# Differential attention on one core: maxima transposed into another bank, values read where the projection left them, squares of the differences on GpSimd

## The reference, cut to what matters

```
Q, K, V = X @ Wq, X @ Wk, X @ Wv            # per head 16 wide; Q, K split into two maps of 8
A1, A2  = Q1 K1^T / sqrt(8), Q2 K2^T / sqrt(8)   (causal)
attn    = softmax(A1) - lam[h] * softmax(A2)
O       = attn @ V                           # 16 wide per head
O       = O / sqrt(mean(O * O) + eps) * rms_scale * 0.2
out     = O @ Wo
```

## Time and profile before

| | us |
|---|---|
| median of 3 runs | 445.51 |
| lowest, highest | 442.61, 448.01 |
| the profiled execution's time | 446.8 |
| its span, first to last instruction | 445.1 |

### The profile page before, as it was taken

The page is one execution under the profiler, slowest core; times in us unless marked ns, Lnnn a source line. Parts: engine busy times, 40 slices in busy tenths (PEclk is TensorE's granted clock), DMA queues, the critical chain, the costliest instruction groups (busy, mean ns, idle before and its releaser), DMA issues.

```text
span 445.1 us, 10136 instructions
## 1 busy us (share of the span) xinstructions
PE 377.5 (85%) x3380; PEld 243.8 (55%) x3380; DVE 288.7 (65%) x952; ACT 259.4 (58%) x634; POOL 203.6 (46%) x324
## 2 busy tenths in 40 slices
PE   0699688795999988888888799897888999999996
PEld 0566487672555545545454455443685566655674
DVE  6586363484889797988889697111132989999200
ACT  3333134133788787787968687877367434343832
POOL 5232224002558575675747475834002687783000
PEclk9999799895999999999999999959899999999999
DMA  8789969984554445152535400000000000000011
GB/s 211 251 275 327 260 145 211 169 157 81 76 74 74 74 75 75 41 91 39 84 45 76 73 4 3 4 1 0 0 2 2 0 0 2 0 0 1 2 48 47
DMA packets 47347, 34.51 MB, mean 78 GB/s; under 512 B 20032, under 2 KB 41664, under 8 KB 47296
## 3 DMA queue, kind: packets, MB, share of 16 engines
q1 hardware_dynamic: 47296, 33.86, 37.2%
HBM read 25.20 MB, written 8.39 MB: 75 GB/s over the span
## 4 chain that ended last, share of the span: by engine, by line
PE 41%; DVE 18%; ACT 11%; issue 11%; DMA 7%; POOL 6%; SPq 5%; DVEq 0%; POOLq 0%
PE ps L1268 5%; PE ps L1088 5%; ACT arena L820 4%; PE ps L1010 4%; DVE arena L1402 3%; DMA stacks<-arena 3%; PE ps L644 3%; DMA qk_parts<-qk_parts_sb 3%; PE ps L1259 2%; PE ps L1018 2%; DVE arena L1415 2%; PE ps L1164 2%; SPq L407 2%; PE ps L1005 2%; PE ps L1134 2%
## 5 line engine op out<-in xcount | busy, mean ns | idle before, releaser
L772 POOL TENSOR_SCALAR_AFFINE_SELECT arena<-arena 128x256 f32<-128x256 f32 (+1 forms) x192 | 90.5, 485 | 88.3 <-ACT arena L820 84.7
L820 ACT ACTIVATE arena<-ps 128x512 f32<-128x512 f32 x192 | 109.3, 604 | 28.7 <-PE ps L1044 27.3
L953 DVE TENSOR_REDUCE arena<-ps 128x4 f32<-128x1024 f32 x64 | 78.2, 1221 | 14.2 <-PE ps L1018 12.9
L946 DVE CUSTOM_DVE_ANT_0 ps<-ps,future 128x128 f32<-128x128 f32 x256 | 66.4, 320 | 22.2 <-PE ps L1005 21.9
L1044 PE MATMUL ps<-stacks 50*128 50x256 bf16 x256 | 50.9, 281 | 1.4 <-ACT arena L820 1.3
L1343 POOL TENSOR_TENSOR arena<-arena 128x1024 f32<-128x1024 f32 x16 | 34.2, 2137 | 34.3 <-DVE arena L1428 33.8
L1010 PE MATMUL ps<-stacks 48*128 48x256 bf16 x256 | 41.7, 277 | 3.4 <-ACT arena L820 2.0
L472 POOL TENSOR_TENSOR qk_parts_sb<-qk_rest,qk_parts_sb 128x512 bf16<-128x512 f32 x16 | 19.1, 1209 | 49.8 <-DVE qk_parts_sb L557 49.8
L1088 PE MATMUL ps<-arena 128*17 128x256 f32 x512 | 41.8, 400 | 0.0
L1005 PE MATMUL ps<-stacks 48*128 48x128 bf16 x256 | 25.3, 220 | 16.2 <-DMA stacks<-arena 7.2
L1471 PE MATMUL ps<-arena,upto 128*128 128x384 f32 x96 | 36.0, 487 | 0.0
(11 more groups left out here) (129 smaller groups left out, 765.0 us busy)
## 6 DMA issues: line engine op xcount, KB each, us to landing
stacks<-qk_parts SPq DMA_DIRECT2D x96, 128.0 KB, 4.5
qk_parts<-qk_parts_sb SPq DMA_DIRECT2D x16, 384.0 KB, 4.5
arena<-in_L_ffn_fc_B_dram SPq DMA_DIRECT2D x4, 1024.0 KB, 8.0
arena<-in_L_ffn_fc_A_dram SPq DMA_DIRECT2D x16, 256.0 KB, 4.8
xs<-in_L_attn_a_X_dram SPq DMA_DIRECT2D x4, 256.0 KB, 3.9
qk_parts<-qk_parts_sb SPq DMA_DIRECT2D x8, 128.0 KB, 5.1
stacks<-arena SPq DMA_DIRECT2D x64, 4.0 KB
out_dram<-xs SPq DMA_DIRECT2D x4, 256.0 KB, 2.3
```

What stands on the lines that cost most here:

```text
L772: nc.gpsimd.affine_select(out=diag, in_=diag, compare_op=ALU.is_ge, fill=0.0, base=0, pattern=[[0, 2 if s < 2 else UMAPS], [1, P]], channe ...
L820: nc.scalar.activation(probs[:, r, s, :], ps[:, bank, :], ACT.Exp, scale=SCALE).then_inc(exp_done, 1)
L946: last = nc.vector.tensor_tensor_reduce(out=block, in0=block, in1=future[:], scale=1.0, scalar=LOWEST, op0=ALU.add, op1=ALU.max, accum_out ...
L953: nc.vector.tensor_reduce(out=rowmax[:, gs, 1, UMAPS * uu:UMAPS * (uu + 1)], in_=ps[:, S_BANK + 1:S_BANK + 3, :].rearrange("p b (m k) -> p ...
```

## The change

The transposed maxima go to columns 256 to 511 of bank 6 (for the first group still to bank 7). With this the wait of L1134 for `shift_lo` goes, and stands ahead of the products of the next slot (slots 1 and 5), which write bank 6. L1112 waits for the copy out of bank 6 (L838) in place of the one out of bank 7 (L847). The copy of the values is dropped and TensorE reads `values`. The squares are a product on GpSimd in slot 2, behind that slot's masks, and the division by 16 is the scale of the Ln.

In order: the lag of the squares; the new home; `attend_gpsimd`, behind the subtraction; `attend_scalar`, where `squares` and its two calls go too; `weigh_values` at t = 0; and `emit` of `attend_tensor`, at the transposes of the maxima and then of the products.

```
-L_DEN, L_DIFF, L_SQ, L_MS, L_ROOT, L_NORM, L_OPT, L_OPROJ, L_STAT = 16, 17, 19, 19, 20, 21, 22, 23, 23
+L_DEN, L_DIFF, L_SQ, L_MS, L_ROOT, L_NORM, L_OPT, L_OPROJ, L_STAT = 16, 17, 18, 19, 20, 21, 22, 23, 23
...
+        def maxima_home(it, j):
+
+            if not past(group(it, j, L_SHIFT)):
+                return ps[0:GMAPS, M_BANK, 0:SEQ]
+            return ps[0:GMAPS, O_BANK + 1, SEQ:2 * SEQ]
...
+                b = seq(it, j, L_SQ)
+                if (j - L_SQ) % UPS == 0 and live(b, SEQS):
+                    pool.wait_ge(post, FIRST + 4 * b + 4)
+                    if past(b):
+                        pool.wait_ge(nT_done, FIRST + b)
+                    nc.gpsimd.tensor_tensor(o_n, o1, o1, op=ALU.mult).then_inc(sq_done, 1)
...
-                b = seq(it, j, L_VAUG)
-                if (j - L_VAUG) % UPS == 0 and live(b, SEQS):
-                    if past(b - 1):
-                        act.wait_ge(pv_done, UPS * (b - 1))
-                    nc.scalar.copy(vaug[:, (j - L_VAUG) // UPS % 2].rearrange("p t h d -> p t (h d)"),
-                                   values[:, bass.ds(TPS * b, TPS), :, :].rearrange("p t h d -> p t (h d)"))\
-                        .then_inc(vaug_done, 1)
...
-                    nc.scalar.activation(msum, msum, ACT.Ln, bias=eps[:, 0:1]).then_inc(ms_log, 1)
+                    nc.scalar.activation(msum, msum, ACT.Ln, scale=1.0 / DV, bias=eps[:, 0:1]).then_inc(ms_log, 1)
...
-                    if jj % UPS == 0:
-                        pe.wait_ge(vaug_done, seq(it, j, L_PV) + 1)
+                    g = group(it, j, L_SHIFT)
+                    if (j - L_SHIFT) % UPG == 1 and live(g, GROUPS):
+                        pe.wait_ge(shift_lo, g + 1)
...
-                    if past(shifts_before(it, j)):
-                        pe.wait_ge(shift_lo, shifts_before(it, j))
-                    transposes_copied(it, j)
+                    if past(g):
+                        pe.wait_ge(shift_lo, g)
+                    if past(unit(it, j, L_PV)):
+                        pe.wait_ge(ot_copied, unit(it, j, L_PV))
...
-                    if (j - L_SHIFT) % UPG == 0 and live(g, GROUPS):
-                        pe.wait_ge(shift_lo, g + 1)
```

More of the change, by code:

```diff
@@ L31 @@
 DV = 2 * DH
-ROOT_OF_INV_DV = 0.25
 MAPS = 2 * HEADS
@@ L68 @@
 PROBS = 4
-L_SHIFT, L_EXP, L_PV, L_OT, L_VAUG = 4, 6, 8, 9, 5
-L_DEN, L_DIFF, L_SQ, L_MS, L_ROOT, L_NORM, L_OPT, L_OPROJ, L_STAT = 16, 17, 19, 19, 20, 21, 22, 23, 23
+L_SHIFT, L_EXP, L_PV, L_OT = 4, 6, 8, 9
+L_DEN, L_DIFF, L_SQ, L_MS, L_ROOT, L_NORM, L_OPT, L_OPROJ, L_STAT = 16, 17, 18, 19, 20, 21, 22, 23, 23
 def live(index, count):
@@ L167, in hybrid_kernel @@
         b2, at = carve(at, (KR, D))
-        vaug, at = carve(0, (2, TPS, HEADS, DV + 1))
-        rowmax, at = carve(at, (2, TPS, GMAPS))
+        rowmax, at = carve(0, (2, TPS, GMAPS))
         shift, at = carve(at, (2, SHIFT_ROWS, SEQ), BF16, GMAPS)
@@ L661, in project_tensor @@
             pe.wait_ge(v_done, SEQS)
-        vaug_done = sem("vaug_done")
         cleared = sem("cleared")
@@ L717, in seq @@
             return (SLOTS // UPS) * it + (j - lag) // UPS
-        def shifts_before(it, j):
-            return (SLOTS // UPG) * it + (j - L_SHIFT - 1) // UPG + 1
+        def maxima_home(it, j):
+            if not past(group(it, j, L_SHIFT)):
+                return ps[0:GMAPS, M_BANK, 0:SEQ]
+            return ps[0:GMAPS, O_BANK + 1, SEQ:2 * SEQ]
         def attend_sync(sp):
@@ L824, in emit @@
                         if s == 0:
-                            squares(it, j)
                             inverse_root(it, j)
@@ L893, in shift_high @@
                         act.wait_ge(shift_in[(k - 2) % 4][h], 32 * (it + (k - 2) // 4 + 1))
-                nc.scalar.activation(shift[:, k % 2, 0, :], ps[0:GMAPS, M_BANK, 0:SEQ], ACT.Copy,
+                nc.scalar.activation(shift[:, k % 2, 0, :], maxima_home(it, j), ACT.Copy,
                                      scale=-1.0).then_inc(shift_hi, 1)
@@ L916, in shift_low @@
                     nc.vector.scalar_tensor_tensor(
-                        out=shift[:, k % 2, 1, :], in0=ps[0:GMAPS, M_BANK, 0:SEQ], scalar=-1.0,
+                        out=shift[:, k % 2, 1, :], in0=maxima_home(it, j), scalar=-1.0,
                         in1=shift[:, k % 2, 0, :], op0=ALU.mult, op1=ALU.subtract).then_inc(shift_lo, 1)
@@ L1075, in weigh_values @@
                 jj = j - L_PV
-                p, r, v = jj % PROBS, jj % 2, jj // UPS % 2
+                p, r, tile = jj % PROBS, jj % 2, TPS * seq(it, j, L_PV) + t
                 if t == 0:
@@ L1087, in weigh_values @@
                     if t == 0:
-                        nc.tensor.matmul(ps[32 * m:32 * m + DV + 1, O_BANK + r, 0:SEQ], vaug[:, v, 0, head, :],
+                        nc.tensor.matmul(ps[32 * m:32 * m + DV + 1, O_BANK + r, 0:SEQ], values[:, tile, head, :],
                                          probs[:, p, m // 2, m % 2 * SEQ:m % 2 * SEQ + SEQ],
@@ L1092, in weigh_values @@
                         last = nc.tensor.matmul(ps[32 * m:32 * m + DV + 1, O_BANK + r, P:SEQ],
-                                                vaug[:, v, 1, head, :], probs[:, p, 2, m * P:(m + 1) * P],
+                                                values[:, tile, head, :], probs[:, p, 2, m * P:(m + 1) * P],
                                                 start=False, stop=True, skip_group_check=True)
@@ L1107, in emit @@
                     pe.wait_ge(maxed, BANKS_U * UPG * (g + 1))
-                    if past(shifts_before(it, j)):
-                        pe.wait_ge(shift_lo, shifts_before(it, j))
-                    transposes_copied(it, j)
+                    if past(g):
+                        pe.wait_ge(shift_lo, g)
+                    if past(unit(it, j, L_PV)):
+                        pe.wait_ge(ot_copied, unit(it, j, L_PV))
                     for t in range(TPS):
-                        last = nc.tensor.transpose(ps[0:GMAPS, M_BANK, t * P:(t + 1) * P],
+                        last = nc.tensor.transpose(maxima_home(it, j)[:, t * P:(t + 1) * P],
                                                    rowmax[:, k % 2, t, :], ident[:])
@@ L1120, in emit @@
                 if live(n, UNITS):
-                    g, b = group(it, j, L_SHIFT), seq(it, j, L_OPT + 1)
-                    if (j - L_SHIFT) % UPG == 0 and live(g, GROUPS):
-                        pe.wait_ge(shift_lo, g + 1)
+                    b = seq(it, j, L_OPT + 1)
                     if (j - L_OPT - 1) % UPS == 0 and live(b, SEQS):
```

## The result

| | us |
|---|---|
| before, median of 20 runs | 444.49 (440.82 to 448.01) |
| after, median of 20 runs | 447.07 (442.85 to 450.41) |
| ratio after to before | 1.0062, 95% interval 1.0037 to 1.0086 |
| forecast, over 445.5 | 447.8, +2.25 |

The change costs 2.6 us by the medians, 0.6%. The interval leaves out 1, so it is slower here, but by little. (Ratios leave out the runs over 1.5% above the fastest of their kernel; the medians have all.) The profiled execution after has a span of 443.9 us against 445.1 before, so the two traces can't be subtracted from each other as wholes; they are compared stretch by stretch.

The account below looks back on a forecast made before the run. The loop was taken as bound by VectorE's gapless shift and maxima plus the shift transfer, not L1134. Terms -0.3 - 2.0 + 3.0 + 0.9 + 0.65 = +2.25 us gave 447.8 us; range 440.5 to 452.5.

Parts of the forecast that it names:

- the clock: Whole run: a half-clock stretch gone or added moves the time some 4 us either way; counted only in the range.
- the squares: Product on GpSimd in slot 2 comes late: +3.0 us in six sequences, +0.9 and +0.65 us in the last two.
- the two gains: New bank -0.3 us and dropped copy of the values -2.0 us, together -2.3 us.
- The bank: L1134's removed wait starts no step of the loop earlier; -0.3 us, for the first groups.
- The values: Copies on ScalarE go, 0.31 us in slot 6 of three sequences and more early on: -2.0 us, bounds 0 and -4.8.
- The squares in the loop: GpSimd's square, taken as 1.27 us, delays L934, then L916 and the transfer: +3.0 us for six sequences, bounds 0 and +5.
- The cover ahead of slot 6: Some 0.3 us of each loss from the late square is taken up ahead of slot 6; bounds 0 and 0.5.
- The tail: Seventh sequence: L872 waits for L934, which waits for GpSimd, +0.9 us; eighth: 1.27 in place of 0.63, +0.65.
- Rival 1: L1134's removed stall was on the path: about 432.5 us; chance 0.07.
- Rival 2: GpSimd's square ends before L934's old start, only the gains are left: about 442 us; chance 0.13.
- Rival 3: GpSimd becomes the bound in slots 2 to 5; each 0.1 us more costs 0.8, 452.8 us at 1.9; chance 0.18.
- the masks of slot 3: GpSimd's masks, needed by slot 5's products, come 1.27 us later with 0.5 us of cover; more would stop slot 5.

Follow-up runs that it names:

- second measurement: The changed kernel timed again against the kernel before, beside three versions with moved statistics: 447.01 us, ratio 1.0024 (0.9980 to 1.0069).
- e1_bank: The kernel before with the new bank for the transposed maxima alone: 443.22 us, ratio 0.9961 (0.9927 to 0.9996).
- e9: New bank and values read directly, squares on ScalarE, new statistics moved from slot 7 to slot 6 of the next sequence; against the kernel before 438.40 us, ratio 0.9852.
- e4_bank_values: The changed kernel with the squares back on ScalarE in slot 3, bank and values as changed; against the kernel before 443.43 us, ratio 0.9932.
- e2_values: The kernel before with the copy of the values dropped alone: 440.75 us, ratio 0.9910 (0.9875 to 0.9944).
- e10: Values read directly and statistics moved to slot 6, squares on ScalarE, without the new bank; against the kernel before 437.39 us, ratio 0.9851.
- e3_squares: The kernel before with the squares on GpSimd in slot 2 alone: 447.98 us, ratio 1.0055 (1.0019 to 1.0091).
- e5_double: The changed kernel with the product of the squares done twice on GpSimd: 459.44 us, ratio 1.0361 to the kernel before.
- e6_sum_later: The changed kernel with the sum of the squares one slot later, Ln and Exp in slot 5: 442.71 us, ratio 0.9973 to the kernel before.
- e8_again: The changed kernel measured once more against the kernel before: 447.01 us, ratio 1.0024 (0.9980 to 1.0069).
- e7_bank_values_sum_later: Bank and values as changed, squares on ScalarE in slot 3, their sum one slot later; against the kernel before 442.27 us, ratio 0.9972.
- e12_stat_sum_later: Bank and values as changed, squares on ScalarE, statistics in slot 6, sum of the squares one slot later; against the kernel before 436.63 us, ratio 0.9883.

## Why the prediction was right

- **The sign and size.** Forecast +2.25 us, measured +2.6. The range, 440.5 to 452.5, holds 447.07. That the two numbers lie so near is in part luck. At equal clock the change costs +0.4 us (give or take 0.9). In the second measurement, the one that has the clocks of both kernels, most of the excess goes with a lower mean clock. The sum had no term for the clock; it stands only in the range. What the sum had too high was the squares: 4.55 us in all, where 2.9 show at equal clock. It had the two gains right, 2.3 against 2.5.
- **The bank: nothing in the loop.** Right. The stall went from L1134 to the scores of slots 1 and 2, with the same sum, and e1_bank's sequence is 24.16 us. What had been read was that VectorE ran without a gap; e9 shows that this was the bound, by taking work out of it. The total of e1_bank, -1.7 us, or -1.5 at equal clock, is more than the -0.3 I took, and no run shows where it comes from; on top of the dropped copy (e4_bank_values against e2_values, e9 against e10) the bank gives nothing.
- **The values: -2.0 us.** The mechanism was right, since the copy stood ahead of slot 6's exponentials and L1132 starts 3.16 us after slot 6. The size was about right too: e2_values gave -4.0 us (-2.5 to -5.6) as measured, but -2.6 at equal clock, of which the steady sequences show 1 to 2.
- **The squares in the loop: +3.0.** GpSimd late, VectorE standing, the shift late by as much, the transfer then on the path: each step stands in the trace. The duration was wrong. I took 1.27 us from L805 and the square took 1.04, so VectorE's wait came out at 0.6 and not 0.9 us. The cover ahead of slot 6, taken as 0.3, was 0.3. By the trace of the change this term is 0.3 a sequence, about +1.5 us; in e3_squares a steady sequence is 0.45 longer, and between e4_bank_values and the change 0.15. All that the squares did, loop and tail, was +2.5 us alone as measured (+3.1 at equal clock). On the other two parts (e4_bank_values to the change) it was about 1.3% as measured, by two comparisons whose intervals leave 0.7 to 1.9%, and 2.9 us at equal clock. So the forecast was right in its mechanism, and too high in this size.
- **The tail: +0.9 and +0.65.** L858 waited 1.47 us for the sum. What that costs the seventh sequence is plain only at full clock: from its subtraction to the first activation of the block behind it took 11.04 us in e3_squares and 10.43 in e2_values, so +0.6. From the start of the subtraction to that of the sum the last sequence took 2.41 us (307.68 less 305.27) where it took 1.96 (308.95 less 306.99): +0.45, again by the shorter square. Together 1.05 us in place of 1.55.
- **Rival 1** (the stall was on the path, 432.5 us) fell with e1_bank. **Rival 2** (GpSimd in time) fell with the 0.60 us wait, though the square of 1.04 us put it nearer than I gave it. **Rival 3** (a longer square) fell, since the squares took 1.04 to 1.05 us each in the loop; but its law is borne out by e5_double: 8.5 us over before at equal clock and some 8 over the change for 1.12 us, near the 0.8 for each 0.1 us, with the half-clock stretches on top.
- **Masks of slot 2 and products of slot 4.** I had cost only the masks of slot 3. TensorE, no longer held by ScalarE ahead of slot 4, arrives there early and stands 0.38 us for GpSimd's masks. It cost nothing, since the shift hangs on VectorE.

## What to carry to other kernels

A long wait of the busiest engine is worth removing only if what releases its next instruction is not the same engine: ask which engine has no gap in that stretch, and take work from that one. Here 1.0 us of statistics moved within VectorE's own list gave 0.8 us a sequence, and a removed stall of 1.1 us gave none. Compare the clocks before you compare the times: a difference of 0.005 in the mean granted clock went with 1.4 us, more than the 0.4 that the change shows at one clock. Work moved from an engine with little slack to one that is idle on average can still come late, if a chain on the idle engine already ends just ahead of its reader; and a reader on an in-order engine should stand behind what others wait for.

## What had not been expected

- A product on GpSimd whose two inputs are the same tile took 1.04 us for 128x512 (f32), against 1.28 for the subtraction of two different tiles beside it and 1.08 for products with one broadcast input. The same operand twice is the likely reason; operation and operands were not varied one by one.
- The transfer of the shift rows landed late now and then in nearly every trace: slot 6 started 2.99 us after L902 in the sequence shown, and up to 3.6 in others of the same kernel. Before, slot 6 had 0.3 us of cover for that.
- With waits longer by 1.1 us a sequence there were four half-clock stretches in a loop that had none (e5_double); e6_sum_later's trace has one there too, at 195.1 us, in a sequence of 25.82 us. The long stretch early in the tail came and went between executions: 10.2 us before, 13.7 after and 6.8 in e8_again, which is the same kernel, and none there in those of e2_values, e3_squares, e7_bank_values_sum_later and e12_stat_sum_later. What decides it stays open.
